# A two-layer decoder with scan, attention and routed experts: four equal groups of batches, a first table of nine tiles, bias products moved off TensorE

## The reference, cut to what matters

```python
# 1. a scan over the 16 batches: a small net is trained by one gradient step per batch
def step(params, x):                      # params W1 (32x128), b1 (32), W2 (128x32), b2 (128)
    z = x @ t_k.T; y = x @ t_v.T
    grads = grad(mean((z + gelu(z @ W1.T + b1) @ W2.T + b2 - y) ** 2))
    new = params - 0.001 * grads
    return new, recon(new, x @ t_q.T)
# 2. cross attention, 16 heads of 8, to the context; out @ Wo.T + bo
# 3. router: top 2 of 8 experts by x @ W_router + b_router; softmax over the two;
#    out = sum over the two of weight * (relu(x @ W1[e] + b1[e]) @ W2[e] + b2[e]),  W1[e] 128x512
# 4. self attention with distance bias      5. cross attention with a mask
# 6. a second layer of 8 experts, top 2, of the same shape
```

## Time and profile before

| | |
|---|---|
| median of 3 runs | 731.08 us (730.79 to 738.47) |
| the profiled execution | 735.26 us, of which the span is 733.3 us |
| mean granted TensorE clock over the span | 0.857 of full speed |
| busy share | TensorE 83%, VectorE 68%, ScalarE 59%, GpSimd 50% |
| prelude | 0 to 62 us |
| first loop | 62 to 284 us |
| first experts | 284 to 371 us |
| second loop | 371 to 627 us |
| second experts and output | 627 to 733 us |

### The profile page before, as it was taken

The page is one execution under the profiler, slowest core; times in us unless marked ns, Lnnn a source line. Parts: engine busy times, 40 slices in busy tenths (PEclk is TensorE's granted clock), DMA queues, the critical chain, the costliest instruction groups (busy, mean ns, idle before and its releaser), DMA issues.

```text
span 733.3 us, 18722 instructions
## 1 busy us (share of the span) xinstructions
PE 608.8 (83%) x6234; PEld 488.1 (67%) x6234; DVE 498.9 (68%) x1443; ACT 433.6 (59%) x897; POOL 367.3 (50%) x666
## 2 busy tenths in 40 slices
PE   2897999999999775999927999997897865799970
PEld 1485677777777554899914767665665644699970
DVE  7653558666767754755526999986899986566546
ACT  1453368667668223798714676765686844488840
POOL 5711424554477746766652433322465866576650
PEclk9897559788779665999958999999899997699995
DMA  7239984000000003222173000000000000322215
GB/s 200 36 111 326 325 300 178 2 1 3 1 16 17 20 19 73 63 76 71 46 249 136 1 3 3 2 2 1 2 2 6 24 20 30 74 81 70 74 37 169
DMA packets 41823, 52.62 MB, mean 72 GB/s; under 512 B 11023, under 2 KB 36865, under 8 KB 41441
## 3 DMA queue, kind: packets, MB, share of 16 engines
q1 hardware_dynamic: 37185, 42.07, 19.1%
q0 software_dynamic: 4544, 9.35, 3.8%
HBM read 40.97 MB, written 28.22 MB: 94 GB/s over the span
## 4 chain that ended last, share of the span: by engine, by line
PE 42%; POOL 15%; DVE 13%; issue 12%; DMA 3%; ACT 1%; SPq 1%; POOLq 0%; DVEq 0%; ACTq 0%
PE p_pT L1450 9%; POOL yo L1616 9%; PE p_s L1436 6%; PE p_o L1476 5%; PE p_o L1481 4%; PE p_s L1427 2%; DVE x_prob L1132 2%; POOL to_row L1611 2%; POOL xs L1085 2%; DVE x L1678 2%; DVE x_inv L1139 1%; PE p_in L1407 1%; DVE x_top L1122 1%; PE p_in L1401 1%; PE p_o L1490 1%
## 5 line engine op out<-in xcount | busy, mean ns | idle before, releaser
L1685 ACT ACTIVATE own_scores<-pack 128x1156 f32 x59 | 68.9, 1167 | 20.1 <-DVE back L1656 12.4
L1085 POOL DMA_INDIRECT xs<-send,x_index x64 | 64.2, 1003 | 18.1 <-issue 16.1
L1347 ACT ACTIVATE x_pT<-p_pT 128x512 f32<-128x512 f32 (+1 forms) x96 | 49.0, 525 | 31.2 <-PE p_pT L1450 29.0
L1730 PE MATMUL p_s<-back,own_scores 128*128 128x128 f32 x472 | 66.1, 286 | 0.0
L1450 PE MATMUL p_pT<-sq,x_prob 128*128 128x128 f32 x320 | 60.1, 319 | 2.5 <-ACT x_pT L1347 1.6
L1730 PEld LDWEIGHTS p_s<-back,own_scores 128*128 128x128 f32 x472 | 60.9, 202 | 0.1
L1122 DVE TENSOR_REDUCE x_top<-p_s 128x12 f32<-128x924 f32 (+2 forms) x48 | 46.9, 1006 | 12.8 <-PE p_s L1436 12.6
L1616 POOL DMA_INDIRECT yo<-own_scores,to_row x39 | 38.1, 977 | 29.7 <-POOL to_row L1611 20.9
L1616 POOL DMA_INDIRECT yo<-back,to_row x39 | 38.1, 977 | 27.7 <-POOL to_row L1611 21.4
L1339 ACT ACTIVATE x_prob<-x_prob 128x1024 f32<-128x1024 f32 x64 | 42.7, 715 | 15.4 <-DVE x_prob L1132 15.2
L1649 DVE TENSOR_SCALAR back<-p_s,own_scores 128x128 f32<-128x128 f32 x118 | 35.9, 345 | 22.1 <-PE p_s L1730 22.0
(11 more groups left out here) (281 smaller groups left out, 1709.1 us busy)
## 6 DMA issues: line engine op xcount, KB each, us to landing
xs<-in_blank SPq DMA_DIRECT2D x2, 8707.5 KB, 43.6
pack<-in_pack SPq DMA_DIRECT2D x16, 578.0 KB, 30.0
back<-xs SPq DMA_DIRECT2D x78, 64.5 KB, 2.3
back<-yo SPq DMA_DIRECT2D x16, 256.0 KB, 4.4
x<-in_x SPq DMA_DIRECT2D x4, 256.0 KB, 4.5
xs<-send,x_index POOLq DMA_INDIRECT x64, 2.4
out<-x SPq DMA_DIRECT2D x4, 256.0 KB, 2.3
yo<-back,to_row POOLq DMA_INDIRECT x39, 2.3
```

Of the source, the lines that this page charges most:

```text
L1085: nc.gpsimd.indirect_dma_start(m["xs"][q][:, :], bass.IndirectOffsetOnAxis(index[:, j, b:b + 1], 0), send[:, b, j, :], None).then_inc(scat ...
L1347: nc.scalar.activation(pT[:, of, :].rearrange("k c q -> k (c q)"), p_pT[:, 0 if beside else g % 2, 0:P * len(sets[g])], ACT.Copy).then_inc ...
L1685: nc.scalar.activation(ws[n % NW], pack[:, bass.ds(e, 1), :].rearrange("p a w -> p (a w)"), ACT.Copy).then_inc(ws_ready, 1)
L1730: ins = mm(p_h[n % 2][k // 2][:, P * (k % 2):P * (k % 2 + 1)], ws[n % NW][:, P * k:P * (k + 1)], xT[:, n % 2, :], start=True, stop=True)
```

## The change

- `GROUPS` becomes (4, 4, 4, 4). The first table comes after eight batches and has 9 tiles, the second has 30. The last group is batches 12 to 15, all of them scattered from the experts' code: one batch after each of the first four stores.
- The transposes of the first two tiles (`first_turns`), their copies (`first_x`) and the products of the first tile (`first_up`) move from the experts' code into the last rounds of the loops: rounds 21 and 22 of the first, rounds 19 and 20 of `x1` in the second.
- TensorE adds no bias in the first loop. `b1r` is held on all 128 partitions (its gradient comes from a product with a full square of ones), and VectorE adds it to a (`add_b1`), behind the maxima in its table; ScalarE's square reads that sum. GpSimd adds bo_x0 to x (`add_bias`).
- The second strip of scores becomes a stage (`score_last`) behind aT.
- The plan of the second table works in other SBUF room.

```diff
-GROUPS = (5, 5, 2, 2, 2)
+GROUPS = (4, 4, 4, 4)
-FIRST_PE = ((3, "score"), (0, "aT"), (1, "aq"), (0, "a"), (4, "tp0"), (5, "po"), (0, "eT"), (2, "turn_in"), (1, "gw2"), (4, "tp1"), (1,
-    "out"), (0, "e_"), (7, "rturn"), (0, "dh"), (4, "tp2"), (8, "rank"), (2, "project"), (0, "g2"), (0, "g1"), (4, "mix"), (0, "g1b"), (7,
+FIRST_PE = ((3, "score"), (0, "aT"), (3, "score_last"), (1, "aq"), (0, "a"), (4, "tp0"), (5, "po"), (0, "eT"), (2, "turn_in"), (1, "gw2"), (4, "tp1"), (1,
+    "out"), (0, "e_"), (7, "rturn"), (21, "first_turns"), (22, "first_up"), (0, "dh"), (4, "tp2"), (8, "rank"), (2, "project"), (0, "g2"), (0, "g1"), (4, "mix"), (0, "g1b"), (7,
     "rlogit"))
-FIRST_DVE = ((5, "scale"), (8, "choose"), (3, "max"), (0, "eTa"), (5, "res"), (1, "w2n"), (0, "slope2"), (0, "slope3"), (1, "comb"), (0,
+FIRST_DVE = ((5, "scale"), (8, "choose"), (21, "first_x"), (3, "max"), (0, "a"), (0, "eTa"), (5, "res"), (1, "w2n"), (0, "slope2"), (0, "slope3"), (1, "comb"), (0,
     "da"), (8, "address"), (8, "plan"), (3, "shift"), (1, "count"), (0, "w1n"), (5, "rcount"), (0, "b1n"), (0, "w2Tn"))
-FIRST_ACT = ((0, "hT"), (1, "hq"), (0, "acopy"), (4, "pT0"), ...
+FIRST_ACT = ((0, "hT"), (1, "hq"), (0, "sq"), (4, "pT0"), ...
-FIRST_POOL = ((2, "rstd"), (2, "norm"), (0, "slope0"), (7, "rnorm"), (0, "slope1"), (9, "scat"), (2, "kT"), (6, "rrstd"))
+FIRST_POOL = ((2, "rstd"), (2, "norm"), (0, "slope0"), (7, "rnorm"), (0, "slope1"), (9, "scat"), (2, "kT"), (3, "bias"), (6, "rrstd"))
...
-        m["scan_b1r"] = sb("scan_b1r", [1, HID])
+        m["scan_b1r"] = sb("scan_b1r", [P, HID])
...
+        own = carve(context[0])
+        m["plan_room"] = [own(REST_TILES * 2 * NE)[0:1] for _ in range(2)]
...
+        def add_b1(b, p):
+            dve.wait_ge(a_ready, b + 1)
+            wait(dve, sq_ready, b)
+            wait(dve, a_safe, b)
+            nc.vector.tensor_tensor(a, p_a, b1r[:, :], ALU.add).then_inc(a_sb, 1)
...
-        def copy_a(b, p):
-            act.wait_ge(a_ready, b + 1)
-            wait(act, da_ready, b)
-            nc.scalar.activation(a, p_a, ACT.Copy).then_inc(a_sb, 1)
-            nc.scalar.activation(a2, p_a, ACT.Square, scale=0.5).then_inc(sq_ready, 1)
+        def square_a(b, p):
+            act.wait_ge(a_sb, b + 1)
+            wait(act, num_done, 2 * b)
+            nc.scalar.activation(a2, a, ACT.Square, scale=0.5).then_inc(sq_ready, 1)
...
-            mm(p_a, zT[:, b, :], w1T[:, :], start=True, stop=False)
-            mm(p_a, ones[0:1, :], b1r[:, :], start=False, stop=True).then_inc(a_ready, 1)
+            mm(p_a, zT[:, b, :], w1T[:, :], start=True, stop=True).then_inc(a_ready, 1)
...
         def grad_w2(b, p):
-            pe.wait_ge(sq_ready, b + 2)
+            pe.wait_ge(a_sb, b + 2)
...
         def turn_e(b, p):
-            pe.wait_ge(sq_ready, b + 1)
+            pe.wait_ge(a_sb, b + 1)
...
-            mm(g_b1r, ones[:, 0:1], da, start=True, stop=True).then_inc(g1b_ready, 1)
+            mm(g_b1r, ones[:, :], da, start=True, stop=True).then_inc(g1b_ready, 1)
...
+        def score_last(b, p):
+            pe.wait_ge(strips_scored, 2 * (b + 1))
+            score_strips(b, p, (1,))
...
-            elif beside:
-                mm(po_out, oT, m["w"](name + "_o"), start=True, stop=False)
-                mm(po_out, m["ones"][0:1, :], m["bo_x0"][0:1, :], start=False, stop=True).then_inc(projected_o, 1)
...
-        last["scatter"](NB - 4)
         place(FIRST)
-        last["scatter"](NB - 3)
         for n in numbers:
             if n + 1 < LAST:
                 place(n + 1)
             store(n)
-            if n == FIRST + 1:
-                last["scatter"](NB - 2)
-            if n == FIRST + 2:
-                last["scatter"](NB - 1)
+            if n - FIRST < LATE:
+                last["scatter"](NB - LATE + n - FIRST)
...
+        def first_turns(b, p):
+            last["banks"]()
+            turn_x(FIRST)
+            turn_x(FIRST + 1)
+        def first_up(b, p):
+            up(FIRST)
```

More of the change, by code:

```diff
@@ L453, in _ @@
                         load(b1c[:, :], t["scan_b1"].rearrange("(p a) -> p a", a=1), ls)
-                        load(b1r[:, :], t["scan_b1"].rearrange("(a p) -> a p", a=1), ls)
+                        load(b1r[:, :], t["scan_b1"].rearrange("(a p) -> a p", a=1).to_broadcast([P, HID]), ls)
                         lm = m["loaded_mask"]
@@ L1089, in gpsimd @@
         if beside:
-            return dict(rstd=rstd_of, norm=norm_in_pool, kT=masked_k, rrstd=route_rstd, rnorm=route_norm_in_pool, scat=scatter)
+            return dict(rstd=rstd_of, norm=norm_in_pool, bias=add_bias, kT=masked_k, rrstd=route_rstd, rnorm=route_norm_in_pool, scat=scatter)
         if own:
@@ L1145, in residual @@
             dve.wait_ge(projected_o, FIRST + b + 1)
-            if not beside:
-                dve.wait_ge(biased, b + 1)
+            dve.wait_ge(biased, FIRST + b + 1)
             nc.vector.tensor_tensor(x[:, b, :], po_out, x[:, b, :], ALU.add).then_inc(res_done, 1)
@@ L1429, in score, with score_strips @@
             pe.wait_ge(k_sb, FIRST + b + 1)
-            for g in (0, 2, 3, 1) if beside else range(NG):
+            score_strips(b, p, (0, 2, 3) if beside else range(NG))
+        def score_last(b, p):
+            pe.wait_ge(strips_scored, 2 * (b + 1))
+            score_strips(b, p, (1,))
+        def score_strips(b, p, groups):
+            for g in groups:
                 r = slice(STRIP * g, STRIP * (g + 1))
-                if beside and g == 1:
-                    pe.wait_ge(strips_scored, 2 * (b + 1))
                 for i0, i1, bank, at in strips[g]:
@@ L1439, in score @@
                     last.then_inc(strips_scored, 1)
-            last.then_inc(scored, 1)
+            if not beside or groups == (1,):
+                last.then_inc(scored, 1)
         def turn_p(groups):
@@ L1658, in vector, with first_x, run, finish @@
         between = ("address", "lengths", "origins", "table")
-        copy_x(FIRST)
-        copy_x(FIRST + 1)
-        last["choose"]()
-        for n in numbers:
-            relu_last(n)
-            if n > FIRST:
-                copy_y(n - 1)
-            if n + 2 < LAST:
-                copy_x(n + 2)
-            if n - FIRST < len(between):
-                last[between[n - FIRST]]()
-            if n == FIRST + FIRST_TILES:
-                weigh()
-        copy_y(LAST - 1)
-        if out is not None:
-            for b in range(NB):
-                dve.wait_ge(y_loaded[b // GT], 16 * 4)
-                for j in range(2):
-                    wait(dve, combined, 2 * b + j)
-                    nc.vector.scalar_tensor_tensor(x[:, b, :], back[:, b, j, :], wts[:, j, b:b + 1], x[:, b, :],
-                                                   ALU.mult, ALU.add).then_inc(combined, 1)
+        def first_x(b, p):
+            copy_x(FIRST)
+            copy_x(FIRST + 1)
+        def run():
+            last["choose"]()
+            for n in numbers:
+                relu_last(n)
+                if n > FIRST:
+                    copy_y(n - 1)
+                if n + 2 < LAST:
+                    copy_x(n + 2)
+                if n - FIRST < len(between):
+                    last[between[n - FIRST]]()
+                if n == FIRST + FIRST_TILES:
+                    weigh()
+            finish()
+        def finish():
+            copy_y(LAST - 1)
+            if out is not None:
+                for b in range(NB):
+                    dve.wait_ge(y_loaded[b // GT], 16 * 4)
+                    for j in range(2):
+                        wait(dve, combined, 2 * b + j)
+                        nc.vector.scalar_tensor_tensor(x[:, b, :], back[:, b, j, :], wts[:, j, b:b + 1], x[:, b, :],
+                                                       ALU.mult, ALU.add).then_inc(combined, 1)
+        return first_x, run
     def scalar(act):
@@ L1741, in down, with run @@
             ins.then_inc(down_done, 1)
-        last["banks"]()
-        turn_x(FIRST)
-        turn_x(FIRST + 1)
-        for n in numbers:
-            up(n)
-            if n + 2 < LAST:
-                turn_x(n + 2)
-            if n == FIRST:
-                last["rank"]()
-            if n == FIRST + 2:
-                last["last_row"]()
-            if n > FIRST:
-                down(n - 1)
-        down(LAST - 1)
+        def first_turns(b, p):
[4 more added lines that the diff above has]
+            up(FIRST)
+        def run():
+            for n in numbers:
+                if n > FIRST:
+                    up(n)
+                if n + 2 < LAST:
+                    turn_x(n + 2)
+                if n == FIRST:
+                    last["rank"]()
+                if n == FIRST + 2:
+                    last["last_row"]()
+                if n > FIRST:
+                    down(n - 1)
+            down(LAST - 1)
+        return first_turns, first_up, run
     def sync(sp):
```

58 lines of the change are left out of this document (34 added, 24 removed).

## The result

The changed kernel takes **751.1 us** (median of 4 runs, 749.2 to 754.8) beside 733.3 of the kernel before on the same chip: ratio 1.024, 95% interval 1.016 to 1.032. Measured again on another chip it is 1.033 (1.025 to 1.042). It is slower; the forecast of 736 stood for +5 us, and +18 came. Medians are over all executions, while each ratio leaves out executions more than 1.5% above the fastest of their kernel, so a ratio is not quite that of the two medians.

What follows compares the result with a forecast made beforehand. The first loop was taken as bound by a ring through VectorE and GpSimd at full clock, by TensorE at low clock. Terms -5.7, +3.7, +0.3, +5.7 sum to +4.0, taken as +5: median 736 us, range 722 to 748.

Steps and rivals of the forecast that it cites:

- the ring: First loop: maxima, add, a to da, back to maxima through VectorE and GpSimd hold full-clock rounds at 10.2 us, before 9.8.
- hidden at 10.2: First loop: GpSimd's add of bo_x0, some 0.5 us, costs nothing within a round of 10.2 us.
- TensorE the bound at low clock: First loop: only at low clock does TensorE's saving count; mixed rounds 14.0 to 12.8 us, first five rounds -2.6 in all.
- the second strip as a stage: First loop: aT moves into the wait for the second strip, saving TensorE 0.24 us per round.
- Two falls: Rounds 8 to 14: two falls of the clock at 2.5 us each give 80.4 against 85.4, so -5.
- the prediction's own sign: First loop: the forecast is wrong if the clock row looks different from the alternation of the kernel before.
- Choices beside the scan: First loop: choices delay round 11 by 4.0 us and round 15 by about 8; round 17 gives 8 back.
- Passage and experts: Experts start 5.6 and 3.6 us earlier; each then loses 7.1 standing still at tile 9 and 2.2 at half clock.
- (a): Rival, first loop: the add isn't late, TensorE's saving comes off all 16 rounds, some -14 us: 727; chance 0.17.
- (c): Rival, experts: nine tiles cover the scatters after all, no standstill: 717 us; chance 0.07.
- (b): Rival, first loop: idle TensorE makes the clock fall more often, five more mixed rounds, +12 us: 748; chance 0.18.
- (d): Rival, first loop: a shorter thin stretch makes the falls of rounds 8 to 14 vanish, -5 more: 731 us; chance 0.13.

Runs made afterwards that it cites:

- run 5: The changed kernel with GpSimd's routing norm moved to the end of its round, one round earlier: 749.6 us, ratio 0.996 to the kernel before.
- run 6: The changed kernel with VectorE adding b1r ahead of the maxima instead of behind them: 742.8 us, ratio 0.984 to the kernel before.
- run 8: The changed kernel with GpSimd adding bo_x0 at the end of its round instead of right behind x_kT: 753.9 us, a single execution.
- run 9: The changed kernel once more, no edit, on another chip: 755.6 us, ratio 1.033 to the kernel before.
- run 4: The changed kernel with batches 12 and 13 scattered ahead of the first store: 742.1 us, ratio 1.009 to the kernel before.
- run 2: The kernel before with only the first loop's edits (b1r on VectorE, bo_x0 on GpSimd, second strips a stage), old groups: 737.6 us, ratio 1.005.
- run 15: The kernel before with the routing norm at the end of GpSimd's round: 733.9 us, ratio 0.995.

## Why the prediction was wrong

**What bounds the kernel, and the ring: right, but too short.** That rounds would not come down to 9.0 because of a ring through VectorE and GpSimd is shown by runs 5 and 6, which shorten it in two places. I had 10.2 for all rounds from 7 to 15. Those before the first scatter take 10.57: maxima and add 1.60 (I had 1.70), add to da 4.58 (4.28), da to the next maxima 4.39 (4.19). The 0.3 is L776 beside the add of bo_x0 (run 8). The add was called "hidden at 10.2", and that failed. The 0.2 is that VectorE does not run "without a gap" from da to the next maxima: it waits 0.39 for TensorE's scores, so the ring closes over g1, mask and scores. Later rounds take 9.98, as there a scatter stands between slope1 and x_kT and both slope instructions run alone. Rounds 5 and 6 were to give 0.1 each and lost 0.14 each. The copies of p_pT were inside the ring, as forecast; once the norm is out of it they are the only wait left on TensorE, in a round of 9.75 (run 5).

**TensorE the bound at low clock: right, but worth less.** A mixed round was to go to 12.8; the one of run 9 with the kernel before's share of low clock takes 13.5. TensorE's busy time in a full-clock round fell by 0.48 (9.57 to 9.09), where 0.83 was added up; the second strip as a stage gave 0.1 instead of 0.24 (mask to L885 took 1.96, to L903 takes 1.87). Rounds 0 to 4 were to give 2.6 and gave 0.7 (1.8 in run 9). Up to round 8 the miss is 4.3 us: 1.9 of it from rounds 0 to 4 and 2.4 from rounds 5 to 7, most of that in round 7, which was partly at half clock (12.13).

**Two falls: the step that failed most.** "7 x 10.2 + 4.0 + 2.5 for each fall of the clock. With two falls, 80.4": rounds 8 to 14 took 86.0. Clean rounds 72.2 of it (0.8 more than forecast), the choice round 5.9 over a clean one (I had 4.0), and 7.9 went to low clock in rounds 8, 9 and 12 (I had 5). This is 5.6 of the miss. I had taken falls away without a reason in the rows: the kernel before has one in four of these seven rounds, and the choice round, in which a fall came too, was priced without one. The price of 2.5 failed with the number. It was that of a fall of some 10 us, and the first fall of these rounds lasted 20 us and cost 6.6 over two clean rounds:

```profile
143.50:163.50 20.00, 19.60 (x156) 14.79 (x156) 11.95 (x42) 11.07 (x22) 8.75 (x19) 0.50 0.01 2
```

Yet rounds 8 to 14 had no lower clock than those of the kernel before, 0.80 against 0.76, which is 34 us at half clock against 41 (first the changed kernel, then the kernel before):

```profile
136.60:222.63 86.03, 77.86 (x720) 58.44 (x720) 57.82 (x205) 55.34 (x119) 45.05 (x85) 0.80 0.02 6
```

```profile
134.72:220.17 85.45, 84.48 (x748) 65.04 (x748) 56.44 (x204) 56.74 (x128) 43.82 (x84) 0.76 0.02 5
```

So there were three falls where the kernel before has four, and the sum had counted on two of 10 us each. That the change made the clock worse is not what the rounds show. Rounds 15 to 17 are the other 1.9: round 16 was partly at half clock (9.96, before 7.63), and round 17 gave 6.4 back instead of 8. In run 9 the miss at round 18 is nearly the same, 11.5 beside 11.8, but lies elsewhere: 1.7 up to round 8, 4.5 in rounds 8 to 14, 5.4 in rounds 15 to 17, whose clock is 0.59. Where the falls come follows no rule that these runs show. By the prediction's own sign (a clock row that does not alternate as before) its account of the clock was wrong. Its reading of the kernel before was wrong in part as well: rounds 5 to 7 are all at full clock there, and the alternation starts with round 8, not with the fourth.

**Choices beside the scan: right that the ring takes them, the sizes partly by luck.** Round 15 takes 7.4 over a clean one (I had 8) and round 11 5.9 (I had 4.0), but both hold some 10 us of half clock, which the forecast left out and which was not measured apart.

**Passage and experts: right.** -7.3 and -2.5 for -5.6 and -3.6; standstills of 7.0 and 7.1 for 7.1, all in all +9.6 and +9.4 for 9.3. The 7.1 is 19.5 - 12.0 less the 0.4 by which TensorE comes later. A side remark was misread: before, tile 13 was loaded 4.7 us ahead of its turn, not 2.7; no term used it. Run 4 shows the cause of the standstills, GpSimd's order. After the wait eight products take 1.92, and in run 4, without the wait, the next tile comes after 1.96.
The rule of the Trainium skill, TensorE: Matmul & The Clock Gate, HAM oscillation, that waits leave the products after them at the slow clock, holds here by both rows.

**The rivals.** (a) is out by the rounds of 10.57, in which g1 waits 0.75 for da, and (c) by the standstills. (b) gave 748, close to the time, but for a cause that isn't shown: it had more falls from the ring's idle time, and run 2, with 1.5 us idle in each round, has a clock of 0.83. That the forecast of the time would have been better with it is luck. (d) is out, as the falls did not vanish. What stays open is why the clock of the kernel before falls in every second round although TensorE idles only 0.2 us in them; run 15 changed neither the 0.2 nor the falls.

## What to carry to other kernels

An engine that is busy all the time may only be filling a dependent pass: before taking work off it, find the two instructions of its queue between which the pass runs, and add up the ring without its filler. An add of 0.2 us moved to another engine is priced by its place in that queue: behind the maxima the round was 0.8 longer than before (0.3 of it from bo_x0 on GpSimd), ahead of them, with two moves on GpSimd, 0.6 shorter. With the scatters' order this turned the change from 1.033 into 0.979, and with groups of 4, 4, 4, 2, 2 into 0.975. A saving that counts on a clock falling less often needs a reason in the rows; without one it is to be forecast with today's falls. A last batch of work that gates a table belongs ahead of stores that nobody waits for yet.

## What the runs showed of the hardware

Two small elementwise instructions on VectorE and GpSimd that start together cost 0.3 us, though neither needs the other: 0.49 for 0.18 (run 8), and 0.40 for 0.13 beside another GpSimd instruction. The kernel before has a median of 733 to 737 us in four groups of runs and of 753 in a fifth; its first loop alone spreads by 13 us between three profiles, by granted clock. A forecast of a few us in such a loop can't be better than that.
